# Loads, six expert matrices and a row of zero products moved in the opening of a fused adapter and transformer kernel

## The reference, cut to what matters

```python
# layer 0, per sequence b
hidden = gelu(x @ down_W.T + down_b)                  # (S, 64)
hidden = hidden @ expert_W[idx[b]].T + expert_b[idx[b]] + domain_emb[idx[b]]
x = layernorm(hidden @ up_W.T + up_b + x) * gamma + beta
# layer 1
emb = silu(sin_emb(timestep)) @ W_ada + b_ada         # scale, shift per sequence
x = layernorm(x) * (1 + scale) + shift
q, k, v = heads(x @ Wq + bq), heads(x @ Wk + bk), heads(x @ Wv + bv)
scores = q @ k.T / 4 + bias                           # (8, 16, 512, 512), masked with -inf
x = x + softmax(scores) @ v @ Wo + bo
out = x + gelu2((layernorm(x) * g2 + beta2) @ W1 + b1) @ W2 + b2
```

## Time and profile before

| | us |
|---|---|
| median of 3 runs (928.11 to 928.75) | 928.49 |
| profiled execution, its own time | 927.84 |
| its span, first to last instruction | 926.0 |
| PE busy | 888.8 (96%) |
| DVE, ACT, POOL busy | 700.5, 717.3, 708.8 (76 to 77%) |

### The profile page before, as it was taken

The page is one execution under the profiler, slowest core; times in us unless marked ns, Lnnn a source line. Parts: engine busy times, 40 slices in busy tenths (PEclk is TensorE's granted clock), DMA queues, the critical chain, the costliest instruction groups (busy, mean ns, idle before and its releaser), DMA issues.

```text
span 926.0 us, 20928 instructions
## 1 busy us (share of the span) xinstructions
PE 888.8 (96%) x6552; PEld 670.5 (72%) x6552; DVE 700.5 (76%) x1892; ACT 717.3 (77%) x1702; POOL 708.8 (77%) x417
## 2 busy tenths in 40 slices
PE   7888889999999999999999999999999999999988
PEld 4665657777777777777777777777777777777766
DVE  6587778788687877878787887878687887675652
ACT  8477889778787878878797787878788787867651
POOL 3966989897697868887887977979687977876700
PEclk9799999999999999999999999999999999999999
DMA  7789789777977689676987779776987669765300
GB/s 213 228 255 326 241 250 318 212 227 206 282 227 231 208 241 307 206 224 201 267 264 222 217 216 287 234 217 207 260 265 220 206 200 274 224 201 179 125 2 23
DMA packets 147039, 206.36 MB, mean 223 GB/s; under 512 B 14249, under 2 KB 61674, under 8 KB 146930
## 3 DMA queue, kind: packets, MB, share of 16 engines
q1 hardware_dynamic: 145538, 203.71, 73.9%
q10 hardware_dynamic: 1392, 1.31, 0.5%
HBM read 183.98 MB, written 20.99 MB: 221 GB/s over the span
## 4 chain that ended last, share of the span: by engine, by line
PE 83%; POOL 4%; DVE 4%; issue 4%; DMA 2%; ACT 2%; SPq 1%; DVEq 0%; POOLq 0%; ACTq 0%
PE tp L1017 20%; PE pv L969 11%; PE la L931 11%; PE sc L1008 11%; PE lc L916 10%; PE lb L703 5%; POOL bias_s L559 3%; PE lb L950 3%; PE lb L719 2%; DMA bias_s<-in_bias 1%; PE la L685 1%; DVE xm L1350 1%; PE lc L677 1%; PE la L665 1%; PE lb L784 1%
## 5 line engine op out<-in xcount | busy, mean ns | idle before, releaser
L559 POOL TENSOR_TENSOR bias_s<-mask_f,bias_s 128x1024 f32<-128x1024 f32 x256 | 601.5, 2372 | 113.8 <-DMA bias_s<-in_bias 112.7
L1675 DVE CUSTOM_DVE_ANT_0 bias_s<-sc,bias_s 128x512 f32<-128x512 f32 x512 | 347.8, 684 | 160.0 <-PE sc L1008 147.1
L1241 ACT ACTIVATE bias_s<-bias_s,mx 128x512 f32<-128x512 f32 x512 | 371.2, 725 | 68.2 <-DVE mx L1675 66.1
L1017 PE MATMUL tp<-ident,bias_s 128*128 128x128 f32 x2048 | 308.3, 273 | 7.1 <-ACT pT L1247 2.7
L1017 PEld LDWEIGHTS tp<-ident,bias_s 128*128 128x128 f32 x2048 | 251.7, 141 | 84.7 <-issue 16.2
L1247 ACT COPY pT<-tp 128x512 f32<-128x512 f32 x335 | 195.3, 583 | 97.7 <-PE tp L1017 95.6
L1008 PE MATMUL sc<-stk,stq 128*128 128x512 bf16 x512 | 195.0, 381 | 6.7 <-DVE mx L1675 6.4
L931 PE MATMUL la<-w_s,act_s 128*128 128x256 f32 x496 | 124.3, 380 | 0.0
L969 PE MATMUL pv<-pT,v_all 128*32 128x256 f32 x2048 | 123.8, 382 | 0.0
L1682 DVE COPY pT<-tp 128x512 f32<-128x512 f32 x177 | 121.2, 685 | 1.9 <-PE tp L1017 1.8
L916 PE MATMUL lc<-hT,w_s 128*128 128x256 f32 x464 | 119.4, 380 | 2.5 <-ACT hT L1194 1.9
(11 more groups left out here) (238 smaller groups left out, 847.5 us busy)
## 6 DMA issues: line engine op xcount, KB each, us to landing
bias_s<-in_bias SPq DMA_DIRECT2D x256, 512.0 KB, 4.6
stq<-q_parts SPq DMA_DIRECT2D x126, 96.0 KB, 4.1
stk<-k_parts SPq DMA_DIRECT2D x124, 96.0 KB, 3.9
k_parts<-kb SPq DMA_DIRECT2D x32, 192.0 KB, 2.3
q_parts<-qb SPq DMA_DIRECT2D x31, 192.0 KB, 2.4
k_parts<-kb SPq DMA_DIRECT2D x32, 128.0 KB, 2.2
stq<-q_parts SPq DMA_DIRECT2D x63, 64.0 KB, 4.7
stk<-k_parts SPq DMA_DIRECT2D x62, 64.0 KB, 4.1
```

Of the source, the lines that this page charges most:

```text
L559: pool.tensor_tensor(tile, mask_f[:, :, :], tile, ALU.subtract).then_inc(s["masked"], 1)
L1017: last = pe.transpose(tp[n % 2][:, kt * P:(kt + 1) * P], bias_s[:, n // 2 % NB, n % 2, kt * P:(kt + 1) * P], ident[:, :])
L1241: act.activation(tile, tile, ACT.Exp, bias=mx[:, t:t + 1], scale=-1.0, accum_out=sums[:, j, head_of(hh):head_of(hh) + 1]).then_inc(s["prob ...
L1675: dve.tensor_tensor_reduce(out=tile, in0=sc[t % 2][:, :], in1=tile, scale=1.0, scalar=BIG, op0=ALU.add, op1=ALU.min, accum_out=mx[:, t:t + ...
```

## The change

SP's list: the second expert's load follows the first; the mask, four biases, w1, x of chunk 2, four biases and wo are issued in front of the other six experts; w2 is issued in the opening, ahead of b2. POOL's list: the mask is converted after the first inverse, and the six experts are formed behind the third head's mask. DVE forms experts 0 and 1 together. PE folds expert 1 into `sc[1]` right after `adapter_up(0)` (ACT copies it), multiplies 7 tiles of zeros between `adapter_down(1, 1)` and `turn_modulation()`, and no longer turns and folds the other six there: the turn is in slot 7 of body 0, the folds in pairs in slots 9, 11 and 13 into bank `lc`, the copies on ACT (8.3) and DVE (10, 12, 14). The experts' tiles lie in `pT[1]` and no longer in `pT[0]`.

```diff
+EXPERTS_AT = dict(turn=7.0, spread=8.3, fold=(9.0, 11.0, 13.0), copy=(10.0, 12.0, 14.0))
...
             load_expert(0, "expert0_in")
+            load_expert(1, "expert0_in")
             load("ada_in", [(w_ada_s, w_ada.rearrange("(c p) n -> p c n", p=P)),
                             (ada_r, b_ada.to_broadcast([P, 2 * D]))])
             load_xt(1)
-            for b in range(1, B):
+            load_mask(0)
+            for n in range(4):
+                load_bias(n)
+            load("w1_in", [(w1_s[:, :, :], w1.rearrange("(c p) n -> p c n", p=P))])
+            load_x(2)
+            for n in range(4, NB):
+                load_bias(n)
+            load("wo_in", [(wo_s[:, :, :], wo.rearrange("(c p) n -> p c n", p=P))])
+            for b in range(2, 5):
                 load_expert(b, "experts_in")
-            load_mask(0)
-            for n in range(3):
-                load_bias(n)
             sp.wait_ge(s["emb_ready"], 1)
             load("emb_out", [(emb_d, emb_s)])
-            load_bias(3)
-            load("wo_in", [(wo_s[:, :, :], wo.rearrange("(c p) n -> p c n", p=P))])
-            for n in range(4, NB):
-                load_bias(n)
-            load_x(2)
+            for b in range(5, B):
+                load_expert(b, "experts_in")
             sp.wait_ge(s["emb_out"], 16)
             load("mod0_in", [(mod0, emb_d[0:1].to_broadcast([P, 2 * D]))])
+            load("w2_in", [(w2_s[:, :, :], w2.rearrange("(c p) n -> p c n", p=P))])
...
             load_bias(NB + 1)
-            load("w1_in", [(w1_s[:, :, :], w1.rearrange("(c p) n -> p c n", p=P))])
...
-                    if i == 0 and t == 16.0:
-                        load("w2_in", [(w2_s[:, :, :], w2.rearrange("(c p) n -> p c n", p=P))])
...
             inverse0(0)
+            convert_mask(0)
             inverse0(1)
             inverse1(0)
-            effective(1, B, 0)
             inverse1(1)
-            effective(1, B, 1)
-            convert_mask(0)
-            for hh in range(4):
+            for hh in range(3):
                 mask_head(0, hh)
+            effective(2, B, 0)
+            effective(2, B, 1)
+            mask_head(0, 3)
             first_residuals()
...
             adapter_up(0)
+            fold_expert(1, sc[1], 0).then_inc(s["fold1_sum"], 1)
             put_rows(1)
...
             adapter_down(1, 1)
+            keep_busy(7)
             turn_modulation()
-            pe.wait_ge(s["eff"], 2)
-            turn_experts(1, B, "turned")
             turn_rows(0)
-            pe.wait_ge(s["spread"], 1)
-            fold_expert(1, tp[1], 1)
...
-            last.then_inc(s["fold_sum"], 1)
             turn_rows(1)
...
+                    if i == 0 and t == EXPERTS_AT["turn"]:
+                        pe.wait_ge(s["eff"], 2)
+                        turn_experts(2, B, "turned")
+                    if i == 0 and t in EXPERTS_AT["fold"]:
+                        fold_late(EXPERTS_AT["fold"].index(t))
...
-            dve.wait_ge(s["fold_sum"], 2)
-            dve.tensor_copy(fold[:, 1, :], tp[1][0:A + 1, D:2 * D])
-            dve.tensor_copy(fold[:, 2:4, :].rearrange("p b d -> p (b d)"), sc[1][0:A + 1, :])
-            dve.tensor_copy(fold[:, 4:6, :].rearrange("p b d -> p (b d)"), lb[0:A + 1, :])
-            dve.tensor_copy(fold[:, 6:8, :].rearrange("p b d -> p (b d)"), lc[0:A + 1, :]).then_inc(s["folded"], 1)
```

53 lines of the change are left out of this document (33 added, 20 removed).

## The result

The changed kernel takes 936.84 us (median of 4 runs, 935.49 to 937.77) against 928.62 for the kernel before in the same comparison (4 runs): 1.0085 times, 95% interval 1.0067 to 1.0103. Measured once more beside later experiments it took 934.97 us against 928.98: 1.0056, 1.0040 to 1.0072. Both say slower, as forecast, but by 6 to 8 us and not by 2.15; both lie above the range's end of 934.5, the second by 0.5 only. The profiled execution took 937.51 us, 9.67 more than that of before.

What follows compares the result with a forecast made beforehand. Most of the span was taken as PE work, with POOL's inverse of chunk 2 limiting the opening's gain. Terms -1.6 + 2.15 + 2.5 - 0.9 = +2.15 gave a median of 930.6 us; range 926.5 to 934.5 (8 in 10).

Steps and rivals of the forecast that it cites:

- term A: Body 0: POOL's inverse of chunk 2 at 54.0, DVE's normalize at 54.05 instead of 55.66: -1.6 us, bounds -2.2 and 0.
- Term B: Body 0, slots 9 to 13: six folds on a nearly full PE, +2.15 us, bounds 1.7 and 3.4.
- B's bound: Body 0: B reaches 3.4 us if DVE's three copies of 0.68 hold a fold up as well.
- Term C: From slot 8.6: PE's clock falls while it stands and stays low into the dense stretch, +2.5 us.
- Term D: Body 1: early w1 and w2 loads remove DVE's two waits for POOL's inverses, -0.9 us, bounds 0 and -3.5.
- POOL's 29.47 us: POOL's work from the second inverse to the end of chunk 2's inverse in the changed kernel, summed at 29.47 us.
- experts late: Rival: DMA at 330 GB/s, last expert near 35, POOL stands 2 to 3 us, A about +0.4: 932.6 us, chance 0.10.
- The opening's gain: Opening: first score tile near 35 instead of 43.09, 8.0 us earlier, without the turns and folds.
- PE's standing: Body 0, before slot 8.6: PE stands some 7 us, from 49.7 to the query projection at 57.0.
- A's upper bound: Term A's bound of 0, with the experts 2 us late.

Runs made afterwards that it cites:

- the run with the experts first: Changed kernel with the loads of experts 2 to 7 right behind the mask's, ahead of all biases: 933.80 us, ratio 1.0052.
- the run without folds: Changed kernel without the six folds on PE in slots 9, 11 and 13, waits and copies kept: 933.43 us, ratio 1.0047.
- that with only the third pair moved: Changed kernel with the third pair of folds at slot 14 instead of 13, its copy at 15, inverse still late: 933.64 us, ratio 1.0052.
- The experiment with slot 14: Third pair of folds at slot 14, its copy at 15: 933.64 us on the changed kernel, 925.58 us with chunk 2's inverse ahead of head 5's mask.
- the one with zeros in the wait: Changed kernel with twelve tiles of zeros on PE right before the query projection of slot 8.6: 933.51 us, ratio 1.0050.
- the early inverse: Chunk 2's first inverse on POOL between the masks of heads 4 and 5, not behind head 7's; on the changed kernel 927.66 us, ratio 0.9990.
- The kernel before with the early inverse: Kernel before with only chunk 2's inverse formed ahead of head 5's mask instead of behind head 7's: 929.38 us, ratio 1.0005.
- the fastest version: Changed kernel with chunk 2's inverse ahead of head 5's mask and the third pair of folds at slot 14, copy at 15: 925.58 us, ratio 0.9957.

## Why the prediction was wrong

The direction was right, and so was the mechanism at the centre: POOL's inverse eats the opening's gain, DVE and then PE stand, and the clock is low. The step that failed is term A: the experts' data were taken to be there at 32.4 us and were there at 35.7. Terms B and C came out too small as well. The ledger, from the two profiled executions, with the stretch at the full clock taken from the experiments:

| | forecast | measured | how |
|---|---|---|---|
| A, query projection against before | -1.6 | +1.57 | 60.16 - 58.59 |
| B, folds | +2.15 | +1.89 | 0.86 ahead of tile 9; 8.47 - 7.44 = 1.03 behind |
| B's bound: DVE's copy holds a fold up | in 3.4 | +1.45 | PE's wait at 71.19 |
| C, low clock | +2.5 | +3.25 | 1.75 from 60.16 to tile 9; 11.42 - 9.92 = 1.50 behind (1.01 in the second trace) |
| tiles 14 to 32 | 0 | -0.44 | 27.53 against 27.97 |
| D, tiles 32 to 64 | -0.9 | -0.89 | 48.73 against 49.62 |
| tiles 64 to 79 | 0 | +2.34 | 27.20 against 24.86 |
| behind tile 79 | 0 | +0.50 | the rest |
| sum | +2.15 | +9.67 | 937.51 - 927.84 |

- **Term A failed, and it is the step that decides.** It rests on the sum of POOL's 29.47 us, which held (29.34 in the run with the experts first), on a start at 24.1, and on 0.4 us of waiting, that is on the experts' data at 32.4. They came at 35.72, and the inverse at 57.19 instead of 54.0, 3.2 us later; A is +1.57 instead of -1.6, by the same 3.2. POOL's own start, 25.41 after DVE had waited 1.37 us for expert 1's data and the clock had fallen in the opening, did not count: in the run without folds and in that with only the third pair moved POOL began at 23.84 and 24.10, as forecast, waited 3.73 and 3.76 us, and had the inverse at 56.91 and 57.21.
- **Why the data came late.** The forecast counted 5.9 MB from the landing of the second sequence of x, at 15.2 in the kernel before. Now that load was issued at 8.96 and took 8.2 us: 17.2, so 2.0 late, and with the forecast's own bytes and rate the sum is 34.6 (an estimate: 17.2, 15.1, 1.3 and 1). The rate was right, 370 to 403 GB/s. The 1.1 us left are about what the sum had no term for: six experts issued by SP at 1 us each, with the store of the embedding between them, while the engines ran dry. The issues of 2.1 us in front of them look like the larger cause, but the engines were full behind them, so they seem to have cost little by themselves; no run separates the two. I had named this rival (experts late, 932.6), at 0.10, with A at +0.4 and all else unchanged.
- **The opening's gain** was 6.42 us at tile 0, not 8. It did not matter: tile 8, at 53.30, was bound by the stk and stq loads, issued at about 47.5 as before, and PE stood 5.43 us at slot 8.6 rather than 7. The forecast had no term for SP's stores and loads between tiles 4 and 8. SP came to them late because it issues, in this order, the six experts, the embedding's loads, w2 and the stores of the keys; in the six traces where I read both, stk's first loads come 12.2 to 12.7 us behind the embedding's load into `act_s` (35.02 and 47.55 in the change), wherever tile 0 lies between 36.00 and 37.85. So the same list caps what is left of the opening's gain at tile 8. PE's standing was 7.8 us in all, 2.34 of it for this and 5.43 for the inverse.
- **Term B** was 0.26 too high at the full clock, within its bounds. But the 3.4 named as its upper bound came true as well: the third pair at slot 13 waits for DVE's copy of the second (slot 12.0, started at 70.46), which stands behind a normalize, a `find_max` and a query step on DVE. The experiment with slot 14 shows this wait to be removable.
- **Term C** was 0.75 short. The clock fell at 53.1, in the wait for stk and stq in front of tile 8, which the forecast did not have. In four other traces of the change and its variants with the late inverse it fell there or just behind tile 8 too (53.2 to 53.8), before PE stood for the inverse, and in the two that are left in that second wait (55.3 and 55.6). When it comes back hangs on the inverse: in six of these seven traces between 63.5 and 66.8, in the one with zeros in the wait at 57.1, and with the early inverse and 3.55 us of standing at tile 8 at 58.4. The rule of the Trainium skill named in the prediction (TensorE: Matmul & The Clock Gate, section HAM oscillation), that a kernel whose PE waits between bursts pays the warm-up after each wait, agrees with the long waits here; waits of 1.22, 1.72 and 0.67 us at tile 8 brought no fall before 60, and with the early inverse and slot 14 PEclk is 1.00 from 50 to 70. (The prediction put the fall in the kernel before at 23.2 us; the 0.87 of its row, 23.0 to 23.5, makes it 23.4, and nothing rests on that.) The prediction took the zeros to keep the clock up, and their time to be free. In the first trace they ran to 27.3, 1.4 us beyond DVE's result at 25.9; in the second that was not so.
- **Term D** was right to 0.01 in tiles 32 to 64 of the first trace, and by its mechanism: the two waits of DVE are gone, and the gain stands in tiles 32 to 42, in the kernel before with those loads moved too. That the whole stretch came out so near is luck in part, as another fall of the clock in it costs the second trace of the change 1.9 us.
- **Chunk 2** (tiles 64 to 79) I had left alone, and the traces do not tie its +2.34 to the change. In the first trace DVE stood there for POOL's inverse (us in all, times, longest, from 140 to 200):

```profile
DVE la L1365 <- POOL rs L574: 2.4, 1, 2.4
```

Of the fourteen traces in the table seven have no such wait, the second of the change among them, and take 24.83 to 25.13 us for these tiles. The other seven have 1.2 to 2.4 us of it and take 26.06 to 27.21, longer by their wait within 0.2 us. The kernel before with the early inverse is one of them (1.6, 26.49), the fastest version another (2.3, 27.21). What makes POOL late there in some executions is open: it waited 12.1 and 11.7 us for biases from 140 to 200 in the two traces of the change, and only one of them has the wait.

The range was too narrow because A's upper bound was 0 "with the experts 2 us late", where they were 3.3 late, and because B stood in it at 2.15, where with its wait it came to 3.34.

## What to carry to other kernels

Work taken off the critical path is paid out only up to the next engine's in-order list: before shortening a stretch, move whatever stands late in the list of the engine with the thin margin (here one 0.9 us operation of POOL, worth 6 to 9 us), since without it the shorter stretch turns into standing, and the standing into a low clock. Price a reordering of loads from where its queue starts in the new kernel, add the issuing engine's time for many small loads at the end, and look at every load behind them, not only at those that are moved. Where a dense stretch holds a wait of 1.5 us for another engine's copy, moving the consumer by one slot is the cheapest edit there is.
